# The adjacency mix of x as three float32r products of high and low parts

## The reference

```python
x = _layernorm(x + einsum('bnf,nm->bmf', x, adj * adj) + bias)
z_l, z_g, v = x @ W_lang.T, x @ W_grav.T, x @ W_V.T
A_l = max(zn @ zn.T, 0) * not_eye            # zn: rows of z_l divided by their norm
A_g = exp(-d2 / (2 * sigma**2)) * not_eye    # d2: squared distances of the rows of z_g
K = w * rows_to_one(A_l * adj) + (1 - w) * rows_to_one(A_g * adj)
x = _layernorm(x + (K @ v) @ W_O.T)
```

## Time and profile before

| | |
|---|---|
| median of 3 runs | 627.4 us (626.99 to 628.38) |
| span of the profiled execution, first to last instruction | 625.0 us |
| TensorE busy | 614.2 us, 98% of the span |
| VectorE busy | 444.2 us, 71% |
| ScalarE busy | 242.7 us, 39% |
| GpSimd busy | 155.5 us, 25% |

### The profile page before, as it was taken

One profiled execution on the slowest core, in us unless ns is written; L12 is line 12 of the kernel. 1 busy time (PEld: TensorE's weight loads), 2 busy tenths in 40 slices (PEclk: granted clock), 3 DMA queues, 4 the chain that ended last, 5 costly groups with the idle time before them and its releaser, 6 DMA issues.

```text
span 625.0 us, 11961 instructions
## 1 busy us (share of the span) xinstructions
PE 614.2 (98%) x4468; PEld 315.0 (50%) x4468; DVE 444.2 (71%) x940; ACT 242.7 (39%) x413; POOL 155.5 (25%) x159
## 2 busy tenths in 40 slices
PE   9999999999999999999999999999999999999994
PEld 6543545454454545454454545445454545545452
DVE  1759486877868586876868687786858788686564
ACT  2345224333443424434432433344342443443333
POOL 1002205032231403123230503223140312323021
PEclk9999999999999999999999999999999999999999
DMA  8722203434123342423223342312334242302103
GB/s 269 244 44 87 51 1 68 136 53 125 52 62 116 64 134 60 141 42 87 90 50 134 67 134 55 120 51 58 119 67 134 59 143 42 92 17 51 69 2 135
DMA packets 89392, 55.05 MB, mean 88 GB/s; under 512 B 70816, under 2 KB 70816, under 8 KB 89376
## 3 DMA queue, kind: packets, MB, share of 16 engines
q1 hardware_dynamic: 19744, 38.05, 17.9%
q10 hardware_dynamic: 69632, 16.79, 13.4%
HBM read 21.27 MB, written 16.78 MB: 61 GB/s over the span
## 4 chain that ended last, share of the span: by engine, by line
PE 96%; DVE 2%; ACT 1%; POOL 0%; issue 0%; POOLq 0%; ACTq 0%; DVEq 0%
PE proj L359 31%; PE proj L375 27%; PE front L339 9%; PE ps_t L389 7%; PE front L429 4%; PE ps_k L429 4%; PE ps_t L400 3%; PE ps_v L409 2%; PE proj L499 2%; PE proj L529 2%; PE ps_v L416 2%; PE ps_t L499 1%; PE ps_k L329 1%; DVE p_lo L736 1%; PE ps_t L529 1%; DVE y L709 0%
## 5 line engine op out<-in xcount | busy, mean ns | idle before, releaser
L557 ACT ACTIVATE p_hi<-proj 128x512 f16<-128x512 f32 x128 | 75.9, 593 | 118.2 <-PE proj L359 117.7
L736 DVE TENSOR_TENSOR p_lo<-proj,p_hi 128x512 f16<-128x512 f32 x128 | 86.0, 688 | 20.9 <-ACT p_hi L557 17.9
L375 PE MATMUL proj<-m_hi,ht_hi 128*128 128x512 f16 x256 | 97.2, 380 | 0.7 <-DVE p_lo L736 0.7
L375 PE MATMUL proj<-m_hi,ht_lo 128*128 128x512 f16 x256 | 97.0, 379 | 0.0
L375 PE MATMUL proj<-m_lo,ht_hi 128*128 128x512 f16 x256 | 97.0, 379 | 0.0
L1026 POOL TENSOR_TENSOR ve<-mv,eps_ln 128x4 f32<-128x4 f32 x31 | 6.6, 212 | 307.7 <-DVE mv L718 211.5
L562 ACT ACTIVATE u<-proj 128x512 f32<-128x512 f32 x64 | 37.9, 592 | 82.7 <-PE proj L375 82.5
L543 ACT ACTIVATE h_hi<-h 128x512 f16<-128x512 f32 x64 | 36.5, 619 | 69.0 <-DVE h L726 69.0
L1065 POOL TENSOR_TENSOR h_lo<-h,h_hi 128x512 f16<-128x512 f32 x30 | 41.5, 1403 | 84.4 <-ACT h_hi L543 84.4
L359 PE MATMUL proj<-ht_hi,l_grav_hi 128*128 128x512 f16 x160 | 60.6, 379 | 0.6 <-DVE p_lo L736 0.6
L359 PE MATMUL proj<-ht_hi,l_lang_hi 128*128 128x512 f16 x160 | 60.8, 380 | 0.0
(11 more groups left out here) (166 smaller groups left out, 1051.8 us busy)
## 6 DMA issues: line engine op xcount, KB each, us to landing
x_in<-in_x SPq DMA_DIRECT2D x16, 1024.0 KB, 7.1
out<-o SPq DMA_DIRECT2D x15, 1024.0 KB, 5.0
w_raw_lang<-in_L_gnn_W_lang SPq DMA_DIRECT2D x4, 256.0 KB, 3.1
o<-in_L_gnn_W_O SPq DMA_DIRECT2D x1, 1024.0 KB, 10.2
w_raw_grav<-in_L_gnn_W_grav SPq DMA_DIRECT2D x4, 256.0 KB, 10.1
u<-in_L_gnn_W_V SPq DMA_DIRECT2D x1, 1024.0 KB, 12.0
ht_hi<-h_hi ACTq DMA_TRANSPOSE x64, 2.4
ht_lo<-h_lo ACTq DMA_TRANSPOSE x64, 2.5
```

What stands on the lines that cost most here:

```text
L375: mm = pe.matmul(proj[j % 3][:, :], a[g.parity][:, k, p * P:(p + 1) * P], b[:, k, :], start=(n == 0), stop=(n == len(passes) - 1))
L557: act.activation(p_hi[:, j % 4, :, j // 4, :], by_batch(proj[j % 3]), ACT.Copy).then_inc(phi_ready, 1)
L736: dve.tensor_tensor(p_lo[:, j % 4, :, j // 4, :], by_batch(proj[j % 3]), p_hi[:, j % 4, :, j // 4, :], ALU.subtract).then_inc(plo_ready, 1)
```

## The change

`wmix` and each pair of x are split into a part rounded to float32r and the float32r remainder. `mix` becomes three float32r products that accumulate in the same bank: high x high, low weights x high x, high weights x low x. The weights are split once by VectorE. ScalarE writes the high part of x (`x_high`, a copy into `x_hi`), GpSimd the remainder (`x_low`, into `x_lo`). For groups 0 and 1 the split stands in the opening; for group g + 2 it stands at the end of the two engines' iteration of group g. `mix` waits for `xlo_ready` of its pair instead of the load of x, and `reload` waits for the split instead of the mixes. The loop over iterations is shortened by one round, which is written out, so that the last two iterations can leave out the split.

```diff
         x_in = [sb(f"x_in{i}", [P, PAIRS, D]) for i in range(2)]
+        x_hi = sb("x_hi", [P, PAIRS, D], F32R)
+        x_lo = sb("x_lo", [P, PAIRS, D], F32R)
...
             def reload(g):
-                sp.wait_ge(l0_done, g.count(4, 4))
+                sp.wait_ge(xlo_ready, g.count(4, 4))
                 load(Group(g.half + 1, g.parity))
...
             def mix(g, p, first=False):
 
-                if p == 0:
-                    pe.wait_ge(x_loaded[g.parity], g.half * 16 + 16)
+                pe.wait_ge(xlo_ready, g.count(4, p + 1))
                 if p >= 2:
                     pe.wait_ge(y_ready, g.count(4, p - 1))
                 elif not first:
                     pe.wait_ge(h_ready, g.prev().count(4, 1))
-                pe.matmul(front[p % 2][:, :], wmix[:, :], x_in[g.parity][:, p, :],
-                          start=True, stop=True).then_inc(l0_done, 1)
+                passes = ((wmix_hi, x_hi), (wmix_lo, x_hi), (wmix_hi, x_lo))
+                for n, (w, x_part) in enumerate(passes):
+                    mm = pe.matmul(front[p % 2][:, :], w[:, :], x_part[:, p, :],
+                                   start=(n == 0), stop=(n == len(passes) - 1))
+                mm.then_inc(l0_done, 1)
...
         def _(act):
+            def x_high(g, p, first=False):
+                if p == 0:
+                    act.wait_ge(x_loaded[g.parity], g.half * 16 + 16)
+                if not first:
+                    act.wait_ge(l0_done, g.prev().count(4, p + 1))
+                act.activation(x_hi[:, p, :], x_in[g.parity][:, p, :], ACT.Copy).then_inc(xhi_ready, 1)
+
...
                 if first:
+                    for p in range(PAIRS):
+                        x_high(nxt, p)
                     m_high(0)
                 p_high(g, 0, first)
...
                 if has_prev:
                     normalise(before, (3,))
                 u_copy(g, 3)
-
-
+                if split_next:
+                    for p in range(PAIRS):
+                        x_high(nxt.next(), p)
+
+
+            for p in range(PAIRS):
+                x_high(Group(0, 0), p, first=True)
             for k in range(DC):
                 act.wait_ge(gw_done, k + 1)
...
+            dve.wait_ge(dve_const, 3)
+            dve.tensor_copy(wmix_hi[:, :], wmix[:, :]).then_inc(wmix_ready, 1)
+            dve.wait_ge(wmix_ready, 1)
+            dve.tensor_tensor(wmix_lo[:, :], wmix[:, :], wmix_hi[:, :], ALU.subtract).then_inc(wmix_ready, 1)
...
+            def x_low(g, p, first=False):
+                pool.wait_ge(xhi_ready, g.count(4, p + 1))
+                pool.tensor_tensor(x_lo[:, p, :], x_in[g.parity][:, p, :], x_hi[:, p, :],
+                                   ALU.subtract).then_inc(xlo_ready, 1)
+
...
                 if not has_prev:
+                    for p in range(PAIRS):
+                        x_low(g.next(), p)
                     pool.wait_ge(norm_copied, 2)
...
                 inverse_norm(g)
+                if split_next:
+                    for p in range(PAIRS):
+                        x_low(g.next().next(), p)
...
+            for p in range(PAIRS):
+                x_low(Group(0, 0), p)
             ln1(Group(0, 0))
```

More of the change, by code:

```diff
@@ L24 @@
 F16 = mybir.dt.float16
+F32R = mybir.dt.float32r
 ALU = mybir.AluOpType
@@ L146, in resnorm_graph_kernel @@
         wmix = sb("wmix", [P, P])
+        wmix_hi = sb("wmix_hi", [P, P], F32R)
+        wmix_lo = sb("wmix_lo", [P, P], F32R)
         not_eye = sb("not_eye", [P, N])
@@ L204, in resnorm_graph_kernel @@
         l0_done = sem("l0_done")
+        xhi_ready = sem("xhi_ready")
+        xlo_ready = sem("xlo_ready")
+        wmix_ready = sem("wmix_ready")
         y_ready = sem("y_ready")
@@ L314, in run @@
         def run(engine, iteration, back):
[L316 to L320, removed]
+            iteration(Group(0, 0), has_prev=False, has_next=True, split_next=True)
+            with engine.Fori(0, G // 2 - 2) as i:
+                iteration(Group(i, 1), has_prev=True, has_next=True, split_next=True)
+                iteration(Group(i + 1, 0), has_prev=True, has_next=True, split_next=True)
+            iteration(Group(G // 2 - 2, 1), has_prev=True, has_next=True, split_next=True)
+            iteration(Group(G // 2 - 1, 0), has_prev=True, has_next=True, split_next=False)
+            iteration(Group(G // 2 - 1, 1), has_prev=True, has_next=False, split_next=False)
             back(Group(G // 2 - 1, 1))
@@ L444, in back, with iteration @@
                     pe.matmul(last_ku_bank[p][:, :], kt[:, p, :], u[:, p, :], start=(p == 3), stop=True).then_inc(ku_done, 1)
-            def iteration(g, has_prev, has_next):
+            def iteration(g, has_prev, has_next, split_next):
                 first = not has_prev
@@ L506, in _ @@
             gram_of("lang")
-            pe.wait_ge(dve_const, 3)
+            pe.wait_ge(wmix_ready, 2)
             for p in range(PAIRS):
```

## The result

The changed kernel takes 707.7 us (703.97 to 709.76, median of four runs), the kernel before 627.4 (four runs as well): ratio 1.127, interval 1.124 to 1.131. The forecast of 686 was 22 us short, and 707.7 lies inside its range, between cases A (686) and B (714).

What follows compares the result with a forecast made beforehand. The prediction took TensorE, busy without gaps in the steady state, to bound the kernel. To 627.4 us it added 53.3 for waits at 14 group boundaries and 5.2 for the opening: 686 us, range 676 to 716.

Steps and rivals of the forecast that it cites:

- case A: Group boundaries: TensorE waits for x_lo behind ScalarE's last u_copy; net 3.86 us each, 686 us in all; chance 0.70.
- case B: Group boundaries: TensorE's clock falls in the gap, 2.0 us lost each, 714 us in all; chance 0.14 for most boundaries.
- What bounds the kernel: Steady state: TensorE busy all 35.74 us of a group, so any added wait is new time, any shorter product saves.
- the longest rows: Upper sum with x_high at 0.80 and x_low at 1.61: 4.57 us per boundary, 6.9 in the opening, 698 us.
- The float32r pass: Mix on TensorE: a pass costs 0.215 us like f16, saving 0.215 per mix, 13.8 for 64 with operands in time.
- Case C: Mix on TensorE: a float32r pass costs 0.43 us; 715 us in all, or near 790; chance 0.13.
- The opening: Groups 0 and 1: the late split starts project(0) at 51.05 instead of 45.45; net 5.2 us lost.
- Case D: Group boundaries: split ready when TensorE asks, needing x_high ahead of the exponent on ScalarE; 621 us; chance 0.02.

Runs made afterwards that it cites:

- experiments 5 and 6: Changed kernel with both split halves issued far earlier, in the opening too: 620.7 us; the same without the product of low weights and high x: 606.7 us.
- experiment 2: Changed kernel with 15 needless float32 products on TensorE behind the last values projection, filling the gap before the mix: 687.8 us, ratio 1.095.
- experiment 1: Changed kernel with its splits and the wait for x_lo, but the mix again one float32 product: 714.4 us, ratio 1.137.
- experiment 3: Changed kernel with only ScalarE's order altered, the four x_high moved ahead of the exponent: 646.0 us, ratio 1.029.
- experiment 7: Changed kernel with x_low of groups 2 to 15 on VectorE instead of GpSimd, behind its work on the group: 681.8 us, ratio 1.085.

## Why the prediction came out as it did

**What bounds the kernel: right.** With no idle time in the steady state, each wait put before TensorE showed in full, and each shorter product too (experiments 5 and 6).

**The chain, case A: right, each term close.** From the start of the last values record (326.94 in the kernel before, one record ahead of the mix in the earlier trace rows) to x_high: 1.96 us predicted, 1.93 measured; x_high and its handover 0.70 and 0.69; x_low 1.38 and 1.25 here (mean 1.28); the first mix 4.20 and 3.94 after that record. The second mix starts 1.25 behind the first, 1.38 predicted; its wait shows as 0.28 instead of 0.6 to 0.7, because the first mix's records take 0.97 (374.69 to 375.66), not the 0.645 of three spacings. At full clock (experiment 2) the way from that record to project(0) is 5.99, against 1.94 before: 4.05 later, where 4.29 was predicted. Net of the mixes behind project(0) the boundary costs 39.51 - 35.74 = 3.77 (3.86 predicted). Experiment 2 as a whole takes 687.8, 1.8 from the forecast's 686. One bound of the sum was off: the longest rows make 4.50 per boundary and 697 us, not 4.57 and 698.

**The float32r pass: right in kind, too low.** 0.234, not 0.215. So six passes take 1.40 where four records took 1.72: mixes 2 and 3 save 0.32, not 0.43, and all mixes with operands in time save about 64 x 0.153 = 9.8 us, not 13.8. Case C (0.43) is out.

**The clock, case B: the step that failed.** B was a rival at 0.14 and occurred at all 14 boundaries, on top of A's chain. The prediction set the gap of 3.8 us against the 4.2 us of idleness that the earlier trace rows show ahead of one fall, and so left the clock at 1.00. That comparison fails in two ways. First, the end of the gap is not the end of the danger: in the changed kernel the last values record ends at 371.13, the mix starts at 374.69, and the clock falls near 375.6, some 4.5 us after that end, when work had already resumed. Second, the 4.2 us are the delay of one fall and no least time: in experiment 1 falls came 2.2 to 4.8 us after the last record's end, at 8 boundaries before the mix had started. What sets the moment stays open; experiment 2 shows only that without the idle stretch the clock stays up.

B's price was too high: 1.45 per boundary, not 2.0. The prediction set the 20 records of the start-up against weight loads 0.1 apart. The same records at full clock, in experiment 2, start 0.11 apart, so 20 of them need 2.2 and the start-up lost some 1.8; and 0.28 of a boundary's slow stretch fall into the second wait, where they cost nothing. Experiment 2's 687.8 plus 14 x 1.45 is 708.1; measured 707.7. The range held this only because it was drawn up to B and C: A's own longest rows end at 697, so the forecast's mechanism alone would have missed.

**The opening: right up to the clock.** x_high of group 1 starts at 45.33 (45.88 predicted). Timeline of TensorE:

```profile
47.36 0.50 PE L350 MATMUL front<-x_hi,wmix_hi 128*128 128x512 f32 x1 [3.54 <-POOL x_lo L1062]
...
50.04 1.70 PE L470 MATMUL ps_k<-ssq,ones 128*128 128x1 f32 x8
51.60 0.59 PE L371 MATMUL proj<-ht_hi,l_lang_hi 128*128 128x512 f16 x1
```

The mixes end near 50.04 (50.15 predicted), but the sums' product takes 1.56 instead of 0.90 at the low clock, and project(0) starts at 51.60 (51.05). The records stay 0.43 apart up to 54.5, so more is lost behind it: at the first boundary the last values record starts at 84.45 instead of 76.74, 7.7 us late, where 5.2 was predicted.

**Case D: rightly ruled out, and its condition was not enough.** x_high ahead of the exponent (experiment 3) removed the gap, but x_low then ran beside VectorE's two-input operations and took longer. D's 621 was reached (620.7) only when both halves were moved far ahead, in the opening too; two errors in D's sum cancelled: 12.0 us off where 14 x 0.61 = 8.5 came off, and 5.2 on for the opening where moving that split left 1.2.

## What to carry to other kernels

A split "a group ahead" is ahead only if its instructions stand ahead of the late work in each engine's queue; read the place in the queue, not the group's number. Where one engine is busy all the time, price a new gap twice: its length, and the clock behind it, which here cost another 1.45 us after a gap of 3.6 and fell inside the gap in some runs and after work had resumed in others. The length of idleness ahead of one fall in a trace is one case, not a limit below which a gap is safe. Before moving work to an idle engine's idle stretch, look at what its neighbour reads in that stretch.

## What the runs showed of the hardware that was not expected

- A float32r pass of 128x512 takes 0.234 us at full clock, a float16 pass 0.215.
- In the changed kernel the clock fell at 14 of 14 gaps of 3.09 to 3.65 us, 0.5 to 1.0 us after TensorE had resumed work; in experiment 7 at 7 of 13 gaps of 2.94 to 3.02 us, 0.8 to 1.5 us after; in experiment 1 at 14 of 14 gaps, 8 times before work had resumed and as early as 2.2 us after the last record's end.
- VectorE operations on two SBUF tiles took 1.42 to 1.66 us beside GpSimd's subtraction instead of 0.69, and the subtraction 1.58 instead of 1.25.
